# A two-layer decoder block: another issue order, another layout of the up-projection and narrower operands in its first layer

## The chip, the cores and the metric

The kernel runs on one NeuronCore of a Trainium2 chip. The metric is the device time of one execution in microseconds (us), lower is better.

## The reference

The input x has 16 sequences of 128 tokens of 256 features. Two layers follow each other, each an attention and a feed-forward part with a gate in front of its result. Only the first layer (layer 0) matters for this change:

```python
x = x + tanh(g_xattn[0]) * _L0_xattn_ref(_layernorm(x), ctx, causal, padding, Wq, bq, Wk, bk, Wv, bv, Wo, bo)
x = x + tanh(g_ffn[0])   * _L0_ffn_ref(_layernorm(x), w_up, w_down)
...
# attention: 32 query heads of 8 features, 8 key/value heads (groups) of 8 features, 128 x 128 scores
scores = einsum('bgrqd,bgkd->bgrqk', q, k) / sqrt(8)     # masked by causal and padding
out    = einsum('bgrqk,bgkd->bgrqd', softmax(scores), v)
# feed-forward: 256 -> 512 -> 256, both products on 8-bit activations and ternary weights
h = hbitlinear(x, w_up, 8);  h = square(relu(h));  return hbitlinear(h, w_down, 8)
# hbitlinear(x, w) = act_quant(fwht(x)) @ weight_quant(w).T ; fwht is a Walsh-Hadamard transform
```

Layer 1 is a second attention (16 heads of 128 features, self and cross, with values rounded to 8-bit floats) and a mixture of 8 experts, 2 for each token.

## The kernel before

**Stages.** Layer 0 goes over the 16 sequences ("tiles", index i). Its work on a tile is cut into pieces, functions with a short name and an engine. `ORDER0` holds, for each of the five engines, the order written out by hand in which it issues the pieces within one turn of the loop; a sign behind a name shifts the tile (`F6---` in the turn of tile i works on tile i-3, `P3++` on tile i+2), and the number behind a colon is the group g of heads. Each engine issues strictly in this order, and pieces wait for each other by semaphores. So a turn of each engine has the work of one whole tile, and the turns overlap like a pipeline. Turns at the two ends leave out pieces of tiles that don't exist. `MIXED` interleaves the last turns of layer 0 (letter a) with the first steps of layer 1's attention (b) and with the loading of its output weights (c). Behind it layer 1's loop, its routing and its experts follow.

**Pieces of attention.** P1, P2, P2t, P2a: normalise a row, transpose it (TensorE), copy it out. P3 (TensorE, L634 to L641): project v, k and q; `wk` is padded with zeros to 128 columns. P3h, P3v: bias, and a split of each number into two 16-bit halves. OUT, INS, INT, ROW (SyncE): send these parts through DRAM into the layouts that the score products need. S:g (L722, L723): the mask and the scores of group g, two products of 512 columns. MX:g (VectorE, L730): their maxima. NT, NTh, NTl: turn the maxima round; ROW puts them into rows 32 and 33 of `qT`. ST:g (L763, L764): the transposed scores minus the maxima, again a mask product and a product of `kT` with `qT`; both tiles have ROWS0 = 96 rows, of which rows 0 to 23 and 32 to 33 carry numbers and the others add zero. EX:g (ScalarE, L773): exponential. PV:g (L785): probabilities times values, fp32, a stationary operand of 32 columns that stands at columns 32 (g mod 4) of the array:

```python
e.matmul(O[GP * j:GP * j + GP, :], v1[:, p, g, :], prob[:, g % RING0, :, :], start=True, stop=True,
         tile_position=(0, GP * j)).then_inc(pe_PV.sem, 1)
```

In the order before, PV:0 to PV:3 stand directly behind one another and NT behind them, and so do PV:4 to PV:7. OC, OB, NO: copy the result out, transpose, divide. OT, OTa, W, Wv: transpose, output projection, add to x.

**Pieces of the feed-forward part.** F1, F1g, F2, F2t, F2a: normalise and transpose (F2 is L859, F2t L867). F3b, F3, F3q: Hadamard transform and quantisation. F4, F4a: transpose of the 8-bit values. F4u (L946): the up-projection, weights stationary, in 8 products of 128 columns, so that its result is transposed already. F4s: relu and square into `hid`. F5v (GpSimd): two butterflies of the 512-wide transform, the second one written to `hidT`. F6 (L974) to F7v (L1016): the rest of the transform, quantisation, down-projection, add to x.

**Preparing layer 1's weights.** LW, WM, WC, WH, WL load and scale one unit of them in each turn; WL (L1056) and WC (L1043, L1046) are long operations on GpSimd.

**Start.** Groups of loads are tied to pieces: the piece `rest` of ScalarE, 22 DMA issues, stands ahead of P2a of tile 2, and the load of the last twelve sequences ahead of CT of tile 2.

Of the kernel before, what the change touches and what calls it, by code (L numbers as in the profile page):

```python
# [252 lines left out]
def make_more_constants(e, t, made):  # L253
# [21 lines left out]
ROWS0 = 96  # L275
# [15 lines left out]
    "gpsimd": "XB+ F5v-- F1g- MK++ WL+ F3b- VC++ PD+ P1g++++ WC++ F7s-- F4v-",
    "sync": "INS- ROW-- INT- LW OUT CT++",
# [3 lines left out]
def layer0(nc, a, t, ctx):  # L296
# [10 lines left out]
    wq, wk, wv = sb("wq0", [P, KD, D]), sb("wk0", [P, KD, P]), sb("wv0", [P, KD, G0 * HD0])  # L307
# [632 lines left out]
    def _(e, i, p):  # L940
# [10 lines left out]
    def _(e, i, p):  # L951
# [3 lines left out]
        e.wait_ge(g_fly.sem, g_fly.at(i - 1))  # L955
# [3 lines left out]
    def _(e, i, p):  # L959
# [106 lines left out]
    def starting(owner, last):  # L1066
# [3 lines left out]
            ("gpsimd", "P1g", 1, 1): ("blocks",), ("gpsimd", "MK", 0, 0): ("ready",), ("gpsimd", "XB", 0, 0): ("gated",),  # L1070
# [10 lines left out]
    def bounds(owner):  # L1081
# [5 lines left out]
             "v_nl": v_nl, "v_max": v_max, "a_exp": a_exp, "v_part": v_part, "v_o": v_o, "a_q1": a_q1, "v_x2": v_x2, "d_out": d_out}  # L1087
# [98 lines left out]
def layer1_attention(nc, a, t, ctx, bank, places, final, small):  # L1186
# [331 lines left out]
    def _(e, i, b, j, kind):  # L1518
# [3 lines left out]
        if first(i):  # L1522
            spent(e, ("a_q1", "v_x2")[kind])
# [207 lines left out]
def routing(nc, a, t, s, flags, A, S, places, packet, rest_halves):  # L1731
# [295 lines left out]
    for b0, b1 in GROUPS[SOON:]:  # L2027
# [25 lines left out]
    "sync": "aaaaaaaaaaaaabaccccbccbcc",
# [354 lines left out]
```

## Time and profile before

| | us |
|---|---|
| median of 3 runs | 1297.82 (1297.1 to 1300.01) |
| profiled execution, its own time | 1297.1 |
| its span | 1295.3 |
| busy: TensorE matmul, weight load | 1172.4 (91%), 930.4 (72%) |
| busy: VectorE, ScalarE, GpSimd | 1059.1 (82%), 908.2 (70%), 748.6 (58%) |
| last F7v (end of layer 0) starts at | 363.8 |

Of the time of an execution 1.8 us lie outside the span. Matmuls in a row overlap in the profile, so the distance between two starts tells what one costs, not its duration. PE is TensorE, DVE VectorE, ACT ScalarE, POOL GpSimd, SP SyncE.

### The profile page before, as it was taken

How to read it: one execution, taken by the hardware profiler on the slowest of the kernel's cores; microseconds unless marked ns; L12 is line 12 of the kernel's file. 1: busy time of each engine (PE TensorE's matmuls, PEld its weight loads, DVE VectorE, ACT ScalarE, POOL GpSimd, SP SyncE). 2: the span in 40 equal slices, each digit the busy share in tenths (PEclk: the TensorE clock that was granted, in tenths of full speed). 3: DMA queues.
4: the chain of work that ended last, by engine and by line, in shares of the span. 5: the costliest groups of instructions: out<-in, count | busy, mean ns of one | idle time of the engine just before them, and what ended most of it. 6: DMA issues, size and time to landing. Idle time of an engine off the chain costs nothing. (4 is left out here: it accounts for less than half of the span.)

```text
span 1295.3 us, 30618 instructions
## 1 busy us (share of the span) xinstructions
PE 1172.4 (91%) x8917; PEld 930.4 (72%) x8917; DVE 1059.1 (82%) x2479; ACT 908.2 (70%) x3605; POOL 748.6 (58%) x1099
## 2 busy tenths in 40 slices
PE   2599999988899999999999999998999999399992
PEld 2256655644588888888888888886887788279992
DVE  6479999988798888988888899897788887656664
ACT  1166666657899899989989988997888787123331
POOL 3457777776756655665665666565556786313331
PEclk9699999999899999999999999999999999689996
DMA  7444444442130202220220221122211000722325
GB/s 171 92 87 90 90 88 82 82 79 47 56 117 2 87 18 69 86 69 17 86 86 0 86 86 36 50 86 85 71 50 55 30 34 21 293 75 77 90 83 195
DMA packets 145817, 100.47 MB, mean 78 GB/s; under 512 B 68541, under 2 KB 139198, under 8 KB 145728
## 3 DMA queue, kind: packets, MB, share of 16 engines
q1 hardware_dynamic: 134592, 87.28, 26.1%
q0 software_dynamic: 3744, 8.45, 1.8%
q10 hardware_dynamic: 7392, 3.64, 1.0%
q8 instruction: 44, 0.72, 0.2%
q14 instruction: 45, 0.37, 0.1%
HBM read 58.42 MB, written 42.48 MB: 78 GB/s over the span
## 5 line engine op out<-in xcount | busy, mean ns | idle before, releaser
L1418 POOL TENSOR_TENSOR head_rstd<-head_rstd,minus_half 128x4 f32<-128x4 f32 x192 | 223.8, 1166 | 15.1
L1406 ACT ACTIVATE squares<-ps 128x128 bf16<-128x128 f32 x768 | 202.0, 285 | 43.1 <-PE ps L1369 35.8
L1369 PE MATMUL ps<-w_proj_in,xq 128*128 128x512 f16 (+1 forms) x1024 | 210.4, 328 | 6.0 <-ACT headsT L1442 5.4
L1498 POOL TENSOR_TENSOR prob<-prob,rinv 128x512 f32<-128x512 f32 x128 | 140.4, 1098 | 108.5 <-DVE rinv L1493 108.3
L1442 ACT ACTIVATE headsT<-ps,l_hln 128x256 f32<-128x256 f32 (+1 forms) x256 | 168.2, 691 | 30.1 <-PE ps L1433 30.1
L1485 ACT ACTIVATE prob<-ps,nmax 128x128 f32<-128x128 f32 x512 | 182.2, 391 | 10.0 <-DVE nmax L1476 8.5
L1406 ACT ACTIVATION_READ_ACCUMULATOR squares<-ps 128x1 f32 x768 | 165.5, 216 | 0.0
L1426 DVE TENSOR_TENSOR heads_n<-ps,head_rstd 128x512 f32<-128x512 f32 x192 | 131.4, 684 | 25.5 <-POOL head_rstd L1418 25.4
L1369 PEld LDWEIGHTS ps<-w_proj_in,xq 128*128 (+1 forms) x1024 | 100.1, 98 | 53.9 <-issue 9.1
L1469 PE MATMUL ps<-headsT 128*128 128x128 f32 x1024 | 136.6, 277 | 1.0 <-DVE probT L1514 0.4
L1416 POOL TENSOR_TENSOR head_rstd<-head_squares,l_head_eps 128x4 f32<-128x4 f32 x192 | 47.1, 246 | 153.0 <-ACT squares L1406 152.1
L1469 PEld LDWEIGHTS ps<-headsT 128*128 128x128 f32 x1024 | 128.7, 192 | 8.0 <-issue 5.4
L1525 PE MATMUL ps<-probT,v 128*128 128x256 f32 x512 | 132.2, 381 | 0.3 <-DVE x_rows L1016 0.3
L1574 PE MATMUL ps<-w_proj_out,catq 128*128 128x256 f16 x1024 | 122.7, 273 | 3.9 <-DVE catq L1562 3.8
L1433 PE MATMUL ps<-ident,heads_n 128*128 128x128 f32 x768 | 117.1, 275 | 6.5 <-DVE heads_n L1426 6.4
L1485 ACT ACTIVATION_READ_ACCUMULATOR prob<-ps,nmax 128x1 f32 x512 | 118.0, 230 | 0.0
L1476 DVE TENSOR_REDUCE nmax<-ps 128x4 f32<-128x512 f32 x128 | 88.2, 689 | 28.8 <-PE ps L1469 27.0
L1574 PEld LDWEIGHTS ps<-w_proj_out,catq 128*128 128x128 bf16 x1024 | 100.3, 98 | 15.4 <-DVE catq L1562 4.4
L1433 PEld LDWEIGHTS ps<-ident,heads_n 128*128 128x128 f32 x768 | 91.3, 142 | 24.3 <-DVE heads_n L1426 16.7
L1376 PE MATMUL ps<-w_proj_in,ctx_parts 128*128 128x256 f16 x768 | 105.0, 273 | 0.0
L730 DVE TENSOR_REDUCE nmax<-ps 128x4 f32<-128x512 f32 x128 | 84.1, 682 | 24.6 <-PE ps L723 21.9
L2271 POOL DMA_INDIRECT picked<-slots_y,to_row x46 | 44.9, 975 | 99.7 <-ACT slots_y L2261 92.3
(302 smaller groups left out, 2772.3 us busy)
## 6 DMA issues: line engine op xcount, KB each, us to landing
slots<-blank_slot SPq DMA_DIRECT2D x12, 1554.0 KB, 8.5
halves<-half_made SPq DMA_DIRECT2D x32, 256.0 KB, 2.5
w_proj_in<-halves SPq DMA_DIRECT2D x16, 512.0 KB, 10.0
taken<-slots SPq DMA_DIRECT2D x23, 259.0 KB, 3.4
w_out_raw<-in_wprojT SPq DMA_DIRECT2D x8, 512.0 KB, 3.9
half_raw<-in_winT SPq DMA_DIRECT2D x16, 256.0 KB, 2.9
half_raw<-in_woutT SPq DMA_DIRECT2D x16, 256.0 KB, 3.1
q_stack<-q_parts SPq DMA_DIRECT2D x48, 64.0 KB
```

The lines of the kernel that those rows point to most:

```text
L1369: last = e.matmul(out, xq[:, k, which, slot_at], weights(k, hl, c0, n), start=(k == 0 and hl == 0), stop=(k == KD - 1 and hl == 1))
L1376: last = e.matmul(out, cx[:, k, part, slot_at], weights(k, hl, c0, n), start=(k == 0 and part == hl == 0), stop=(k == KD - 1 and part == 1))
L1406: last = e.activation(squares[:, 4 * n + h, :], A[n][:, h * HD1:(h + 1) * HD1], ACT.Square, scale=HD1**-0.5, accum_out=hss[:, 4 * n + h:4 ...
L1418: e.tensor_tensor(hr[:, four], hr[:, four], t["half"][:, four], ALU.pow).then_inc(g_r[n].sem, 1)
L1426: e.tensor_tensor(hn[:, n, :, :], A[n][:, :].rearrange("p (h d) -> p h d", h=4), spread(hr[:, 4 * n:4 * n + 4], HD1), ALU.mult).then_inc(v ...
L1433: last = e.transpose(A[n][:, h * P:(h + 1) * P], hn[:, n, h, :], ident[:, :])
L1442: last = e.activation(hT[:, n, h0:h1, :].rearrange("p h t -> p (h t)"), A[n][:, h0 * P:h1 * P], ACT.Identity, bias=hln[:, c + 1:c + 2], sc ...
L1469: last = e.matmul(S[kind][:, h * P:(h + 1) * P], hT[:, kind, h, :], hT[:, 2, 2 * kind + h // 2, :], start=True, stop=True)
L1485: last = e.activation(prob[:, kind, h, :], S[kind][:, h * P:(h + 1) * P], ACT.Exp, bias=nmax[:, kind, h:h + 1], accum_out=rowsum[:, kind, ...
L1498: e.tensor_tensor(prob[:, kind, :, :], prob[:, kind, :, :], spread(rinv[:, kind, :], P), ALU.mult).then_inc(g_p[kind].sem, 1)
L1525: last = e.matmul(O[kind][:, g * 2 * P:(g + 1) * 2 * P], v[:, kind, g, :], probT[:, kind, 2 * g:2 * g + 2, :], start=True, stop=True)
L1574: last = e.matmul(A[1][:, 0:D], catq[:, 4 * kind + h, :], wp[:, hl, 4 * j + 16 * kind + h, :], start=(n == 0), stop=(n == 15))
```

## The change

- `ORDER0` gets another order on all five engines. On TensorE, PV:4 and PV:5 stay together and the other six PV pieces of a turn stand alone between other products; NT stands alone; P2t moves from two to three tiles ahead.
- The up-projection F4u has the activations stationary: 2 products of 512 columns. Its result isn't transposed, so F5 (4 fp32 transposes into bank F0) and F5a (ScalarE copies 128x512 from there to `hidT`) are new, and F6 waits for F5a. F5v writes its second butterfly back to `hid`. The pieces that use bank F0 (F2t, and near the ends OT and W) wait for F5a as well; in layer 1 the first PV does.
- ROWS0 falls from 96 to 34, so the product of ST has 34 rows; `wk` has 64 columns without padding. Two memsets of 32 rows at the start become one of two rows, and that of `qT` covers 34 rows.
- The pieces that loads are tied to come in the new order: in ScalarE's, P2a of tile 2 stands directly behind P3h of tile 1, where it stood behind WH and NTh of tile 0. The wait for the gates on GpSimd moves from XB to PD.
- `MIXED` has new strings. On TensorE 25 steps of layer 1 stood ahead of layer 0's last piece, now 17.

The diff, cut: the entries `a_hT`, `pe_hT` in the lists of flags and the other strings of `MIXED` are left out.

```diff
-ROWS0 = 96
+ROWS0 = TOP + 2
 
 ORDER0 = {
     "tensor": (
-        "PV:2- PV:3- NT ST:5- P2t++ F6--- ST:6- OB:0- F2t-- ST:7- P3++ S:0+ F3-- PV:4- PV:5- PV:6- PV:7- ST:0 "
-        "S:1+ ST:1 S:2+ F4-- ST:2 OB:1- F4u-- S:3+ ST:3 S:4+ OT- ST:4 S:5+ F7--- W- S:6+ S:7+ F7d--- PV:0 "
-        "PV:1"
+        "S:7 F5--- ST:4- ST:5- OB:0- NT F6--- P3++ F2t-- ST:6- PV:4- PV:5- ST:7- PV:6- S:0+ F3-- PV:7- "
+        "ST:0 ST:1 S:1+ OB:1- S:2+ F4-- ST:2 ST:3 F4u-- PV:0 OT- PV:1 S:3+ S:4+ PV:2 S:5+ F7--- W- "
+        "P2t+++ S:6+ PV:3 F7d---"
     ),
     "scalar": (
-        "EX:5 P2a+++ F2a- EX:6 EX:7 P3h+++ OC:1 EX:0+ EX:1+ F4a- EX:2+ F4s- OTa WH++ F7a-- EX:3+ NTh++ EX:4+ "
-        "OC:0+"
+        "WH EX:7- P3h++ OC:1- EX:0 EX:1 F4a-- EX:2 F4s-- OTa- EX:3 F7a--- OC:0 P2a+++ F5a-- EX:4 NTh+ "
+        "EX:5 F2a- EX:6"
     ),
     "vector": (
-        "MX:5+ Wv- MX:6+ MX:7+ F1- F7v--- WM++ NTl+ F2- F6q-- NO:0 P1++++ MX:0++ F3q- P3v+++ MX:1++ MX:2++ "
-        "NO:1 MX:3++ MX:4++ P2++++"
+        "F2-- NO:0- NTl F6q--- WM+ P1+++ MX:0+ F3q-- NO:1- P3v++ MX:1+ MX:2+ P2+++ MX:3+ MX:4+ MX:5+ Wv- "
+        "F1- MX:6+ F7v--- MX:7+"
     ),
-    "gpsimd": "XB+ F5v-- F1g- MK++ WL+ F3b- VC++ PD+ P1g++++ WC++ F7s-- F4v-",
-    "sync": "INS- ROW-- INT- LW OUT CT++",
+    "gpsimd": "XB WC F5v--- F4v--- F1g-- MK+ F3b-- F7s--- WL VC+ P1g+++ PD+",
+    "sync": "ROW- INT CT++ OUT+ LW+ INS+",
 }
...
-    wq, wk, wv = sb("wq0", [P, KD, D]), sb("wk0", [P, KD, P]), sb("wv0", [P, KD, G0 * HD0])
+    wq, wk, wv = sb("wq0", [P, KD, D]), sb("wk0", [P, KD, G0 * HD0]), sb("wv0", [P, KD, G0 * HD0])
...
-            e.dma_start(wk[:, k, 0:G0 * HD0].rearrange("p (g d) -> p g d", g=G0), one_head).then_inc(w_first, 16)
+            e.dma_start(wk[:, k, :].rearrange("p (g d) -> p g d", g=G0), one_head).then_inc(w_first, 16)
...
         e.memset(kT[0:TOP, :, :, :].rearrange("p s g t -> p (s g t)").bitcast(F32), 0.0)
-        for r0 in range(TOP, ROWS0, 32):
-            e.memset(kT[r0:r0 + 32, :, :, :].rearrange("p s g t -> p (s g t)"), UP)
+        e.memset(kT[TOP:ROWS0, :, :, :].rearrange("p s g t -> p (s g t)"), UP)
         e.wait_ge(x_in[0], 16)
 
     @s.piece("ready", "vector")
     def _(e):
-        e.memset(wk[:, :, G0 * HD0:P], 0.0)
...
         for k in range(KD):
-            e.matmul(X[:, k_at:k_at + P], wk[:, k, :], cT[:, p, k, :],
+            e.matmul(X[0:G0 * HD0, k_at:k_at + P], wk[:, k, :], cT[:, p, k, :],
                      start=(k == 0), stop=(k == KD - 1))
...
@@ OT and W (tensor): the waits for the bank F0, outside the loop @@
-        filling(e, i, (a_yT, -1), (v_x1, -1))
+        filling(e, i, (a_yT, -1), (a_hT, -2), (v_x1, -1))
...
-        filling(e, i, (a_q1, -1), (a_yT, -1))
+        filling(e, i, (a_q1, -1), (a_yT, -1), (a_hT, -2))
...
@@ F2t (tensor) @@
         e.wait_ge(f_yn.sem, f_yn.at(i))
+        e.wait_ge(a_hT.sem, a_hT.at(i - 1))
         filling(e, i, (v_x1, 0), (a_oT, 0), (a_q1, -1))
...
@@ F4u (tensor) @@
-        for m in range(KF):
-            for k in range(KD):
-                last = e.matmul(F1[:, m * P:(m + 1) * P], wup[:, k, m * P:(m + 1) * P], q1T[:, k, :],
-                                start=(k == 0), stop=(k == KD - 1))
+        for k in range(KD):
+            last = e.matmul(F1[:, :], q1T[:, k, :], wup[:, k, :], start=(k == 0), stop=(k == KD - 1))
...
@@ F4s (scalar) @@
-        e.wait_ge(g_fly.sem, g_fly.at(i - 1))
+        e.wait_ge(pe_hT.sem, pe_hT.at(i - 1))
...
@@ F5v (gpsimd), F5, F5a, F6 @@
+        e.tensor_tensor(hid[:, 0:2, :], fly[:, 0:2, :], fly[:, 2:4, :], ALU.add)
+        e.tensor_tensor(hid[:, 2:4, :], fly[:, 0:2, :], fly[:, 2:4, :], ALU.subtract).then_inc(g_fly.sem, 1)
+
+    @s.piece("F5", "tensor")
+    def _(e, i, p):
+        e.wait_ge(g_fly.sem, g_fly.at(i))
+        if not isinstance(i, int) or i + 1 < B:
+            e.wait_ge(v_x1.sem, v_x1.at(i + 1))
+        filling(e, i, (a_oT, 1), (a_q1, 0), (a_yT, 0))
+        for k in range(KF):
+            last = e.transpose(F0[:, k * P:(k + 1) * P], hid[:, k, :], ident[:, :])
+        last.then_inc(pe_hT.sem, 1)
+
+    @s.piece("F5a", "scalar")
+    def _(e, i, p):
+        e.wait_ge(pe_hT.sem, pe_hT.at(i))
         e.wait_ge(pe_h2.sem, pe_h2.at(i - 1))
-        e.tensor_tensor(hidT[:, 0:2, :], fly[:, 0:2, :], fly[:, 2:4, :], ALU.add)
-        e.tensor_tensor(hidT[:, 2:4, :], fly[:, 0:2, :], fly[:, 2:4, :], ALU.subtract).then_inc(g_fly.sem, 1)
+        e.activation(hidT[:, :, :].rearrange("p k t -> p (k t)"), F0[:, :], ACT.Copy).then_inc(a_hT.sem, 1)
 
     @s.piece("F6", "tensor")
     def _(e, i, p):
-        e.wait_ge(g_fly.sem, g_fly.at(i))
+        e.wait_ge(a_hT.sem, a_hT.at(i))
...
@@ PV of layer 1, first step @@
-            spent(e, ("a_q1", "v_x2")[kind])
+            spent(e, ("a_hT", "v_x2")[kind])
...
@@ MIXED["tensor"], layer 0 (a) and layer 1 (b) at the handover @@
-        "aaaaaaaaaaaaaaaaaaaaaaaaaaaaaaaabaaaaaaaaaabaaaaaaaaaaaaaaaaaaabaaaaaaaaaaabbaaaaabaaababaaabbababab"
-        "ababbbbabababbbbababbbbbbbbbbbbbbbbbbbbbbbbbbbbbbbbbbbb"
+        "aaaaaaaaaaaaaaaaaaaaaaaaaaaaaaaaaaaaaaaaaaaaaaaaaaaaaaaaaaaaaaaaaaaaaaaaaaaaaaaaaaaaaaaaaaaaaaaaaaaa"
+        "aaaaaaaaaaaaaaaaaaaaaaaaaaaaaaaaaaaaaaaaaaaaaaaabaaaaaaaaabaaaaaaababaabbaababbabbaabbbaabbbabbbbbbb"
+        "bbbbbbbbbbbbbbbbbbbbbbbbbbbbbbbbbbbbb"
```

## Rows read from the trace of the kernel before

**Rows 1.** Stretches of 40 us: length, busy (instructions) of each engine, clock, DMA, GB/s.

```profile
core 0: us, PE busy (x) PEld busy (x) DVE busy (x) ACT busy (x) POOL busy (x), PEclk, DMA share, GB/s
40.00:80.00 40.00, 27.80 (x140) 13.96 (x140) 22.13 (x47) 13.92 (x27) 16.79 (x21) 0.78 0.44 83
...
160.00:200.00 40.00, 38.46 (x262) 23.24 (x261) 37.05 (x96) 25.46 (x50) 30.87 (x51) 1.00 0.46 91
...
280.00:320.00 40.00, 33.18 (x203) 17.53 (x202) 35.09 (x101) 24.73 (x49) 25.99 (x47) 0.91 0.26 57
```

**Rows 2.** Timeline of PE, 180 to 200 us: start, duration, line, operation, count.

```profile
180.75 0.60 PE L1009 MATMUL ps<-wdn,q2T 128*128 128x256 bf16 x4
181.28 1.07 PE L785 MATMUL ps<-prob,v_ones 128*32 128x512 f32 x8
182.28 0.28 PE L736 MATMUL ps<-ident,nmax 128*32 128x128 f32 x1
182.40 0.38 PE L763 MATMUL ps<-minus,causal_b 128*128 128x512 bf16 x1
182.61 0.38 PE L764 MATMUL ps<-q_rows,k_rows 96*128 96x512 f16 x1
...
184.48 0.60 PE L798 MATMUL ps<-ident,o_cols 128*128 128x128 f32 x4
186.16 0.44 PE L867 MATMUL ps<-ident,yn 128*128 128x128 f32 x2 [1.08 <-DVE yn L859]
...
189.63 1.06 PE L785 MATMUL ps<-prob,v_ones 128*32 128x512 f32 x8
190.62 0.39 PE L763 MATMUL ps<-minus,causal_b 128*128 128x512 bf16 x1
...
192.93 0.60 PE L798 MATMUL ps<-ident,o_cols 128*128 128x128 f32 x4
193.37 0.61 PE L946 MATMUL ps<-q1T,wup 128*128 128x128 bf16 x8
193.86 0.39 PE L722 MATMUL ps<-mask,minus 128*128 128x512 bf16 x1
...
196.50 1.08 PE L834 MATMUL ps<-wo,oT 128*128 128x256 f32 x4
197.41 0.38 PE L722 MATMUL ps<-mask,minus 128*128 128x512 bf16 x1
...
198.29 0.60 PE L1009 MATMUL ps<-wdn,q2T 128*128 128x256 bf16 x4
```

**Rows 3.** Timeline of DVE, same stretch.

```profile
183.91 2.20 DVE L859 SCALAR_TENSOR_TENSOR yn<-x_rows,mv_f,rstd_f 128x256 f32<-128x256 f32 x1
...
196.00 0.48 DVE L597 SCALAR_TENSOR_TENSOR xn<-x_rows,mv_p,rstd_p 128x256 f32<-128x256 f32 x1
```

**Rows 4.** Timeline of POOL, same stretch.

```profile
183.69 2.13 POOL L1056 TENSOR_TENSOR w_proj_in<-unit_raw,w_proj_in 128x1024 f32 x1
```

**Rows 5.** PE by source line L785: duration min/median/max in ns, first and last start.

```profile
L785 PE MATMUL ps<-prob,v_ones x256: 592/617/1062, 65.6 to 331.1; 128*32 128x512 f32 x128
```

**Rows 6.** Timeline of ACT at the start.

```profile
44.23 5.92 ACTq L399 DMA_DIRECT2D wo<-in_WoT  x16
...
53.26 0.38 ACT L617 ACTIVATE xnT<-ps 128x256 f32<-128x256 f32 x1 [8.77 <-issue]
```

**Rows 7.** Timeline of PE at the start.

```profile
53.78 1.08 PE L634 MATMUL ps<-wv,cT 128*128 128x64 f32 x4 [9.17 <-ACT xnT L617]
...
57.33 0.51 PE L722 MATMUL ps<-mask,minus 128*128 128x512 bf16 x1
```

**Rows 8.** Timeline of SP at the start.

```profile
44.93 1.39 SPq L692 DMA_DIRECT2D k_blocks<-k_parts  x4
46.41 1.24 SPq L755 DMA_DIRECT2D q_rows<-most_rows  x2
```

**Rows 9.** Stretches of 7 us where the granted clock falls.

```profile
283.00:290.00 7.00, 3.94 (x18) 1.84 (x15) 6.14 (x25) 1.79 (x3) 3.10 (x7) 0.73 0.27 59
290.00:297.00 7.00, 6.41 (x32) 2.94 (x31) 5.14 (x16) 3.31 (x7) 4.86 (x8) 0.78 0.02 5
```

**Rows 10.** Groups by line and shape, 160 to 240 us: busy, mean ns of one.

```profile
L792 ACT ACTIVATE o_cols<-ps 128x512 f32<-128x512 f32 x9 | 5.3, 590 | 5.8 <-PE ps L785 5.8
```

More of the change, by code:

```diff
@@ L553, in layer0 @@
     v_q1, g_two, pe_q1, a_q1 = sig("v_q1", "vector"), sig("g_two", "gpsimd", 2), sig("pe_q1", "tensor"), sig("a_q1", "scalar")
-    pe_up, a_hid = sig("pe_up", "tensor"), sig("a_hid", "scalar", 2)
+    pe_up, a_hid, pe_hT = sig("pe_up", "tensor"), sig("a_hid", "scalar", 2), sig("pe_hT", "tensor")
     g_sum, g_fly, g_scale = sig("g_sum", "gpsimd"), sig("g_fly", "gpsimd", 2), sig("g_scale", "gpsimd")
-    pe_h2, v_q2 = sig("pe_h2", "tensor"), sig("v_q2", "vector")
+    a_hT, pe_h2, v_q2 = sig("a_hT", "scalar"), sig("pe_h2", "tensor"), sig("v_q2", "vector")
     pe_q2, a_q2, pe_dn, v_x2 = sig("pe_q2", "tensor"), sig("a_q2", "scalar"), sig("pe_dn", "tensor"), sig("v_x2", "vector")
@@ L927, in _ @@
         e.wait_ge(a_yT.sem, a_yT.at(i))
-        filling(e, i, (v_x1, 0), (a_oT, 0))
+        filling(e, i, (a_hT, -1), (v_x1, 0), (a_oT, 0))
         for k in range(KD):
@@ L1069, in starting @@
             ("scalar", "P3h", 0, 0): ("weights",), ("scalar", "P2a", 1, 1): ("gated",), ("scalar", "P2a", 2, 0): ("rest",),
-            ("gpsimd", "P1g", 1, 1): ("blocks",), ("gpsimd", "MK", 0, 0): ("ready",), ("gpsimd", "XB", 0, 0): ("gated",),
+            ("gpsimd", "P1g", 1, 1): ("blocks",), ("gpsimd", "MK", 0, 0): ("ready",), ("gpsimd", "PD", 0, 0): ("gated",),
             ("tensor", "P3", 0, 0): ("ready",), ("tensor", "S", 0, 0, 0): ("late",), ("tensor", "W", 0, 0): ("out",), ("tensor", "F3", 0, 0): ("made",),
@@ L1086, in layer0 @@
     final = {"pe_qkv": pe_qkv, "pe_S": pe_S, "pe_ST": pe_ST, "pe_PV": pe_PV, "pe_OB": pe_OB, "g_mask": g_mask, "g_ulow": g_ulow,
-             "v_nl": v_nl, "v_max": v_max, "a_exp": a_exp, "v_part": v_part, "v_o": v_o, "a_q1": a_q1, "v_x2": v_x2, "d_out": d_out}
+             "v_nl": v_nl, "v_max": v_max, "a_exp": a_exp, "v_part": v_part, "v_o": v_o, "a_hT": a_hT, "v_x2": v_x2, "d_out": d_out}
     layer = Layer(s, lambda owner: starting(owner, bounds(owner)[0]), lambda owner: some(owner, bounds(owner)[1], B + B), turn,
@@ L2040 @@
     "tensor": (
-        "aaaaaaaaaaaaaaaaaaaaaaaaaaaaaaaabaaaaaaaaaabaaaaaaaaaaaaaaaaaaabaaaaaaaaaaabbaaaaabaaababaaabbababab"
-        "ababbbbabababbbbababbbbbbbbbbbbbbbbbbbbbbbbbbbbbbbbbbbb"
+        "aaaaaaaaaaaaaaaaaaaaaaaaaaaaaaaaaaaaaaaaaaaaaaaaaaaaaaaaaaaaaaaaaaaaaaaaaaaaaaaaaaaaaaaaaaaaaaaaaaaa"
+        "aaaaaaaaaaaaaaaaaaaaaaaaaaaaaaaaaaaaaaaaaaaaaaaabaaaaaaaaabaaaaaaababaabbaababbabbaabbbaabbbabbbbbbb"
+        "bbbbbbbbbbbbbbbbbbbbbbbbbbbbbbbbbbbbb"
     ),
     "vector": (
-        "aaaaaaaaaaaaaaaaaabbaaaaaaaaaaaaaabaaabaaaaaaaabaaaaabbbabbbaaaabaababbacbaaacaabbbabbbbbcbcbabbabbb"
-        "abbbbbbbbcbbbbbbbbcbbbbbbbbbbbbbbbbcbbbbbbbbbbbcbbbbbbb"
+        "aaaaaaaaaaaaaaaaaaaaaaaaaaaaaaaaaaaaaaaaaaaaaaaaaaaaaaaaaaaaaaaabbaababaababcaabcbbbbaaacababbabbccb"
+        "abbbabbbbbbabcbbbbbbbbbbbbbbbbbbbbbbbbbbbbbbbbbbbbbbbbbbbbbbbbbbbcbbcb"
     ),
     "scalar": (
-        "aaaaaaaaaaaaaaaaaaaaaaaaaaaaaaaaabbbaaaabaaabaaabaabaabbaabcaaaabaabababaababccbbbacbbbbabababbbccbb"
-        "babbbbbbbbbbcbbbbbbbbcbbbbbb"
-    ),
-    "gpsimd": "aaaaaaaaaaaabaaaaaaaaaaabaaaaaaabbaababababaababaabbbabbabbbbbbbbbbbbbbbbbbbbbbbb",
-    "sync": "aaaaaaaaaaaaabaccccbccbcc",
+        "aaaaaaaaaaaaaaaaaaaaaaaaaaaaaaaaaaaaaaaaaaaaaaaaaaaaaaaaaaaaaaaaaaaacacaaabaabbbabbababaabacbabbabbb"
+        "ccabababbabbbbbabcbbbbbbbbbbbbbbbbbbbbbbbbbbbbbbcc"
+    ),
+    "gpsimd": "aaaaaaaaaaaaaaaaaaaaaaaaaaaaaaaaaaaaaaaaaaaababaabbaaabbaabbaabbabbbbbbbbbbbbbbbbbbbbbbbbbbbbb",
+    "sync": "aaaaaaaabcccbcccccb",
 }
```

## The prediction

> **What bounds the kernel now.** I read the stretches of 40 us first, because the change touches layer 0 alone, which ends near 364 us. In its middle PE is busy for 38.46 of 40 us, DVE for 37.05, ACT and POOL for far less [rows 1]. So two engines are near their limit and the timelines must decide. In PE's the same product comes round from 180.75 to 198.29 us, a turn of 17.54 us [rows 2]. The only gap in it stands ahead of F2t: the four transposes of OB start at 184.48 and four such cost 0.44 us (192.93 to 193.37), the next start is 186.16, so 1.24 us are lost and 16.3 us are work. The gap ends with F2 on DVE, which takes 2.20 us there where the like of it takes 0.48 us [rows 3]; WL of POOL runs for 2.13 us at that time [rows 4]. So DVE is as full as PE only because one operation of it is held up, and behind it PE has a queue of work that barely fits. PE's work in a turn is what I sum.
>
> **PV alone.** A fp32 product of 256 columns costs 0.23 us (four from 196.50 to 197.41), so one of 512 columns some 0.45 us, and a PV is two such instructions, 0.91 us. The eight instructions of four PVs would be 3.6 us in a row; they take 0.99 us from their first start to the next product (189.63 to 190.62) [rows 2]. Four PVs stand at different columns of the array and run side by side; a block lasts as long as one of them. Going in costs a little more: four products at 0.11 us (half the 0.22 us of 512 columns) from 180.75 should end at 181.18, the block starts at 181.28, 0.10 us later; and 0.99 is 0.08 us over 0.91. So a block costs 1.09 us, whether it holds four or one. Before there are 2 in a turn. In the new order there are 7: PV:4 with PV:5, then PV:6, 7, 0, 1, 2 and 3, each with full-width products between, which need the columns that the lone PV uses. Five more blocks are +5.45 us. NT had its place behind a block in the same form (32 columns) and now pays for going in and out itself: 0 to 0.2 us, I take 0.15.
>
> **Switches of form.** The 0.10 us before and 0.08 us behind a block are the one price that the rows show for a change of the form in which the array is used. The product of ST goes from 96 to 34 rows, between products of 128. The trace has no product with 64 rows or fewer; those of 96 rows pay nothing (0.22 us in a row with 128 rows, 182.61 against 182.40) [rows 2]. Its bounds are 0 and, by the block of 32 columns, 0.18 us, 8 times in a turn: 0 or +1.45 us. I take the upper end, as 34 rows fit into half of the array like 32 columns into a quarter, and 96 don't; that is a guess from the nearest row. The Trainium skill (TensorEngine Tiling (Array Packing), Key Properties) says that changing the tiling mode drains the engine, and lists 64 rows as a mode of its own; the block of 32 columns agrees with it (0.10 and 0.08 us), and by that rule these are the +1.45 us. The page TensorE: Matmul & The Clock Gate of the Trainium skill (LDWEIGHTS) says that the number of rows makes no difference to a weight load; by that alone it would be 0.
> `wk` with 64 columns is between +0.2 us (a switch) and -0.2 us (four loads of half the width); I take 0.
>
> **The feed-forward part.** F5 is four fp32 transposes, +0.44 us like OB's. F4u takes 0.49 us now (193.37 to 193.86) and two products of 512 columns take 0.43: -0.05. F5a is one more ACT copy of 128x512, 0.59 us [rows 10] on an engine that is busy for 25.46 of 40 us; with PE's turn over 20 us it is hidden. If it were not, PE would wait at F6, but OB, NT and two STs (2.2 us) stand between F5 and F6. F5v is the same work to another tile.
>
> **The sum of a turn:** 5.45 + 0.15 + 1.45 + 0.44 - 0.05 = +7.45 us, from 16.3 to 23.8 us of PE work. DVE (37.05 of 40 us, so 16.3 us of a turn with the held-up F2 in it) then has 7 us of slack, POOL more. So F2's hold-up, which the new order may end (WL now stands behind F3b and F7s, and F2 waits for F1g alone), saves nothing. I followed the waits round one turn with the durations above (maxima to S two groups later; F3q to F4; OC to OB; F5v to F5; NT by ROW's two transfers to ST:0): each has more PE work in front than it lasts, the narrowest ROW with 2 us to spare. 16 tiles: +119 us.
>
> **What is taken off.** PE's idle time is filled. From the first S of tile 1 (57.33) [rows 7] to the last PV instruction (331.1) [rows 5] are 274 us. Work in them: 16 x 16.3 = 261 us, less some 19 of first and last pieces outside, plus 4 of layer 1's steps, 246 us; so 28 us idle, of which 6.8 lie in 280 to 320 us [rows 1]. I estimate that 10 remain (start, and turns near the end with less work): -18 us.
> The start: the 22 issues of `rest` hold ACT until 53.26, 8.77 us, and P3 of tile 2 and S:0 of tile 1 behind it start at 53.78 and 57.33 [rows 6, 7]. In the new order `rest` follows P3h of tile 1, which is done at 27 us, when ACT has nothing to do. S:0 of tile 1 then waits for INS, whose last issue starts at 44.93 for 1.39 us [rows 8]; LW stands before it now (six issues, 2.7 us). I expect it near 50 us: -7 us; bounds -9 and 0.
> The handover: layer 0's last tile has F5 and F5a in its chain, 1.4 us with their waits, and 8 steps of layer 1, about 6 us of PE work that filled gaps, come after it. Some of that overlaps: +6 us.
>
> **Sum:** 119 - 18 - 7 + 6 = +100 us on the profiled execution's 1297.1 us, which is 0.7 us under the median: **1398 us** for a median.
>
> **Rivals.**
> A, narrow rows are free. The product of 34 rows costs what 96 did. For it: 96 rows cost the same as 128. Against it: what 32 columns pay. 119 falls by 23 to 96 us: 1375 us. Chance 0.22.
> B, the clock. Half-clock stretches appear where PE waits: 0.73 and 0.78 between 283 and 297 us behind a gap of 3 us [rows 9]. Five blocks more in which a quarter of the columns works could let it fall in the middle of layer 0, where it is 1.00 now [rows 1]. Against it: PE never rests. If a tenth of the 380 us of PE work ran at 1.2 instead of 2.4 GHz, +38 us: 1436 us. Chance 0.10.
> C, the other side: a lone PV doesn't block. If full-width products start in the other columns while a PV runs, as other PVs do, six lone PVs cost little over their share of a block (0.25 us), and a turn is 16.3 + 0.44 + 0.15 + 1.45 = 18.3 at most; without the switches 16.9, under today's 17.54. With the hold-up of F2 gone the period falls by 0.3 us and the start by 7: 1286 us. It decides where a lone PV costs under 0.4 us. Against it: the product behind a block starts 0.99 us after it, never within it. Chance 0.05.
> D, another wait in the new order (ROW or F5v late) comes on top of PE's work, 1 to 2 us a turn: 1415 us. Chance 0.08.
> The forecast itself: 0.55, with a range of its own of 1380 to 1415 us.
>
> **How the numbers follow.** The range takes the forecast, A and D with the bounds of the start and the idle time, and leaves out C and most of B: 1355 to 1422 us. About 0.2% is what a measurement can tell from no change. Only C isn't slower: 0.04 for faster and 0.01 for within 0.2%, where its parts are eaten up; the other four are slower, 0.95.
>
> **What would show it.** In the profile after, layer 0 ends near 463 us and a turn of PE is near 23.8 us without gaps over 1 us; each lone PV takes 1.0 to 1.1 us from start to next start; ST's second product is followed or preceded by 0.1 us more than S's; ACT has no `rest` issues at 44 us; busy DVE falls to two thirds in the middle. Layer 1 and the experts are as before. Wrong would be: lone PVs under 0.5 us, a turn that ends with a wait of PE for another engine, a granted clock under 1.00 in the middle of layer 0.

## The result and the profile after

The changed kernel takes 1393.47 us (median of 4 runs, 1390.16 to 1395.96), the kernel before beside it 1298.91 (1297.1 to 1302.65). The ratio is 1.072, with a 95% interval of 1.0697 to 1.0742. The profiled execution took 1393.06 us, its span is 1390.6, so 95.3 us more than before.

I read the stretches first, for they answer whether PE became the only bound. Changed kernel, columns as in [rows 1]:

```profile
160.00:200.00 40.00, 40.00 (x178) 16.73 (x177) 26.08 (x70) 20.66 (x39) 24.52 (x39) 1.00 0.35 71
```

PE is busy for 40.00 us of 40 with 178 matmuls where it had 262; DVE fell from 37.05 to 26.08 us [rows 1]. PE is full, with fewer instructions, so each must cost more. Timeline of PE in the changed kernel, which answers to [rows 2] (its lines are 1 or 2 lower up to F5 and 12 higher behind it; L783 is PV, L761 and L762 are ST, L720 and L721 are S, L734 is NT, L632 to L639 are P3, L944 is F4u, L971 F5, L1021 F7d):

```profile
237.24 0.28 PE L929 MATMUL ps<-ident_b,q 128*128 128x128 bf16 x2
237.35 0.38 PE L761 MATMUL ps<-minus,causal_b 128*128 128x512 bf16 x1
237.66 0.39 PE L762 MATMUL ps<-q_rows,k_rows 34*128 34x512 f16 x1
237.99 0.39 PE L761 MATMUL ps<-minus,causal_b 128*128 128x512 bf16 x1
238.31 0.39 PE L762 MATMUL ps<-q_rows,k_rows 34*128 34x512 f16 x1
238.62 0.60 PE L944 MATMUL ps<-wup,q1T 128*128 128x512 bf16 x2
239.16 1.05 PE L783 MATMUL ps<-prob,v_ones 128*32 128x512 f32 x2
240.14 0.44 PE L817 MATMUL ps<-ident,o_rows 128*128 128x128 f32 x2
240.50 1.04 PE L783 MATMUL ps<-prob,v_ones 128*32 128x512 f32 x2
241.48 0.39 PE L720 MATMUL ps<-mask,minus 128*128 128x512 bf16 x1
...
245.77 1.04 PE L783 MATMUL ps<-prob,v_ones 128*32 128x512 f32 x2
246.75 0.61 PE L1021 MATMUL ps<-wdn,q2T 128*128 128x256 bf16 x4
...
247.63 0.60 PE L971 MATMUL ps<-ident,hid 128*128 128x128 f32 x4
248.07 0.38 PE L761 MATMUL ps<-minus,causal_b 128*128 128x512 bf16 x1
...
249.83 0.27 PE L734 MATMUL ps<-ident,nmax 128*32 128x128 f32 x1
249.94 1.06 PE L986 MATMUL ps<-had,hidT 128*128 128x128 f32 x8
250.83 0.56 PE L632 MATMUL ps<-wv,cT 128*128 128x64 f32 x4
251.32 0.65 PE L635 MATMUL ps<-cT,wk 128*64 128x128 f32 x4
...
252.90 0.38 PE L866 MATMUL ps<-ident,yn 128*128 128x128 f32 x2
...
253.74 1.05 PE L783 MATMUL ps<-prob,v_ones 128*32 128x512 f32 x4
254.73 0.39 PE L761 MATMUL ps<-minus,causal_b 128*128 128x512 bf16 x1
...
270.41 0.61 PE L1021 MATMUL ps<-wdn,q2T 128*128 128x256 bf16 x4
```

A turn, from F7d to F7d, is 270.41 - 246.75 = 23.66 us, and no start in it has an idle time beside it. A lone PV (two instructions) holds PE for 0.98 us (239.16 to 240.14, 240.50 to 241.48), the pair (four) for 0.99 (253.74 to 254.73), as eight did before. The steps between ST's products are 0.31, 0.33, 0.32 and 0.31 us (237.35 to 238.62) where they were 0.21 to 0.22.

The start, in the timelines of ACT and PE, answers to [rows 6, 7]; the last three rows are PV, F7v (L1028) and F2 (L857) by source line, with their first and last start:

```profile
25.36 4.91 ACTq L399 DMA_DIRECT2D wo<-in_WoT  x14
```

```profile
41.28 0.66 PE L632 MATMUL ps<-wv,cT 128*128 128x64 f32 x4 [0.66 <-DMA cT<-in_ctxT]
...
49.30 0.61 PE L720 MATMUL ps<-mask,minus 128*128 128x512 bf16 x1 [5.08 <-DMA k_blocks<-k_parts]
```

```profile
L783 PE MATMUL ps<-prob,v_ones x256: 592/617/1061, 56.6 to 413.3; 128*32 128x512 f32 x128
...
L1028 DVE SCALAR_TENSOR_TENSOR x_rows<-ps,quant,x_rows x16: 464/484/484, 129.1 to 452.2; 128x256 f32<-128x256 f32 x10, 128x256 f32 x6
L857 DVE SCALAR_TENSOR_TENSOR yn<-x_rows,mv_f,rstd_f x16: 466/475/486, 84.8 to 424.3; 128x256 f32<-128x256 f32 x16
```

The first S of tile 1 starts 8.0 us earlier (49.30 against 57.33). Layer 0 ends 88.4 us later (452.2 against 363.8) and the span 95.3, so 6.9 us arise behind it. F2 (L857) takes 486 ns at most; its hold-up [rows 3] is gone, and the turn is longer all the same.

### The profile page after: what moved, and what is told of

Read it like the earlier page. It is cut to its first block and busy times, and to the rows that moved or that the text cites. A ratio compares the mean times of both kernels' runs of the same rounds, so it can differ in the third digit from the quotient of the medians.

```text
span 1390.6 us, 30539 instructions
## 1 busy us (share of the span) xinstructions
PE 1286.4 (93%) x8885; PEld 938.2 (67%) x8885; DVE 1054.3 (76%) x2477; ACT 925.3 (67%) x3621; POOL 743.8 (53%) x1099
## 5 line engine op out<-in xcount | busy, mean ns | idle before, releaser
L1438 DVE TENSOR_TENSOR heads_n<-ps,head_rstd 128x512 f32<-128x512 f32 x192 | 131.3, 684 | 25.0 <-POOL head_rstd L1430 24.8
L783 PE MATMUL ps<-prob,v_ones 128*32 128x512 f32 x256 | 116.0, 612 | 0.1
```

The costliest lines, as they stand in the source:

```text
L1438: e.tensor_tensor(hn[:, n, :, :], A[n][:, :].rearrange("p (h d) -> p h d", h=4), spread(hr[:, 4 * n:4 * n + 4], HD1), ALU.mult).then_inc(v ...
```

## The experiments

Each run has the kernel before beside it (medians 1298.45 to 1299.14 us). Every ratio is to that.

**Wide operands again**, in the changed kernel: `ROWS0 = 96`, `wk` of 128 columns with its padding.

> The changed kernel with only the narrow operands undone: ROWS0 is 96 again, wk has 128 columns with zeros, the memsets of before are back. Theory 1 (TensorE's work sets the turn, and each change of form costs 0.1 us each way): in the trace after, the mask product to ST's product takes 0.32 us and ST's product to the next one 0.32 us, against 0.22 with 96 rows, and wk's four stand 0.09 us later at both ends. That is 8 x 0.20 + 0.18 = 1.8 us a turn, 29 us for 16 tiles, less 1 to 3 us for the longer memsets at the start: 1364 to 1368 us. Theory 2 (the new order's waits set the turn and not TensorE's work): the time stays within 5 us of 1393.

Measured: 1365.01 us, ratio 1.0513 (1.0484 to 1.0541), 28.5 us less than the changed kernel. A turn of PE is 21.92 us here (239.24 to 261.16, from PV:6 to PV:6) against 23.66, and 16 times the difference of 1.74 us is 28 us. The narrow operands cost what the switches add up to; rival A is out.

**66 rows instead of 34**, `wk` left narrow:

```diff
-ROWS0 = TOP + 2
+ROWS0 = 66
```

> The changed kernel with ROWS0 66 instead of 34, and nothing else: rows 34 to 65 add zeros. In the changed kernel's trace a product of 34 rows costs 0.10 us more on its way in and 0.10 us on its way out than S's of 96 rows, 8 times a turn and 16 turns, 25.6 us. Theory 1 (the product is slow because it fits into half of the array's rows and the array changes its form for it): 66 rows don't fit, the 25.6 us go, 1366 to 1370 us. Theory 2 (any product with another number of rows than its neighbour pays, or pays by how few they are): 1380 us or more. a_wide took back 34 rows and 64 columns together and gave 28.5 us, so what is left of it to the 64 columns of wk is 28.5 less this run's gain: some 3 us by the trace's 0.18 us a turn.

Measured: 1368.69 us, ratio 1.0539 (1.0514 to 1.0563), 24.8 us less. Timeline of PE in this run:

```profile
234.91 0.61 PE L1022 MATMUL ps<-wdn,q2T 128*128 128x256 bf16 x4
...
236.67 0.38 PE L762 MATMUL ps<-minus,causal_b 128*128 128x512 bf16 x1
236.88 0.38 PE L763 MATMUL ps<-q_rows,k_rows 66*128 66x512 f16 x1
237.10 0.60 PE L797 MATMUL ps<-ident,o_cols 128*128 128x128 f32 x4
...
257.10 0.61 PE L1022 MATMUL ps<-wdn,q2T 128*128 128x256 bf16 x4
```

Steps of 0.21 and 0.22 us: 66 rows cost what 128 cost, 34 cost 0.1 us more on each side. So it isn't that neighbours differ in rows. A turn is 22.19 us (234.91 to 257.10), 1.47 less than with 34 rows; the other 0.27 us of the 1.74 belong to `wk`. At which number between 34 and 66 the price begins wasn't tried. The Trainium skill (TensorEngine Tiling (Array Packing), Key Properties) says that changing the tiling mode drains the engine; 34 against 66 rows agrees with it, if 34 rows run in a mode of fewer rows than 66.

**Narrow operands in the kernel before**, the reverse of the first run, so `ROWS0 = TOP + 2` and `wk` of 64 columns.

> The kernel before with only the narrow operands of the change: ROWS0 34, wk of 64 columns, the memsets of after. Theory 1: 1.8 us of TensorE work more in a turn that has 1.2 us of idle time in it, so +10 to +25 us: 1308 to 1323 us, ST's product starts 0.32 us behind its mask product. Theory 2 (VectorE sets the turn before, switches are hidden under it): within 5 us of before, 1294 to 1304 us.

Measured: 1318.17 us, ratio 1.0145 (1.0117 to 1.0172), +19.0. The same operands cost 28.5 us where PE is full and 19.0 where a turn has waits. Part of the difference is seen: between 120 and 280 us PE waits for other engines and for loads for 6.3 us in the kernel before and for 4.1 here. The rest wasn't traced.

**PV pieces apart in the kernel before**, seven blocks in a turn instead of two, all else as it was:

```diff
-"PV:2- PV:3- NT ST:5- ... S:0+ F3-- PV:4- PV:5- PV:6- PV:7- ST:0 ... S:6+ S:7+ F7d--- PV:0 PV:1"
+"PV:2- ST:5- PV:3- NT ... S:0+ PV:4- PV:5- F3-- PV:6- ST:0 PV:7- ... S:6+ PV:0 S:7+ PV:1 F7d---"
```

> The kernel before with only TensorE's order altered so that the PVs stand in 7 blocks instead of 2 (PV:4 with PV:5, the other six alone, NT behind PV:3), nothing else. Theory 1: 5 x 1.07 = 5.35 us of work more in a turn, 86 us for 16 tiles, of which 15 to 20 us fill idle time: 1361 to 1373 us. Theory 2 (a product of full width can run beside a lone PV): under +20 us, and in the trace a product that follows a lone PV starts less than 0.5 us behind it.

Measured: 1364.33 us, ratio 1.0498 (1.0469 to 1.0527), +65.2. Stretch of this run:

```profile
160.00:200.00 40.00, 39.99 (x214) 19.83 (x216) 28.74 (x78) 21.84 (x44) 25.92 (x42) 1.00 0.30 65
```

PE full, DVE down to 28.74 us: this edit alone makes the picture of the changed kernel in its middle. Five blocks by 1.07 us and 16 tiles are 86 us. The 20 us that are missing went into idle time by this sum, as the expectation had it (15 to 20).

**PV pieces together in the changed kernel**, in two blocks of four, the rest of the new order kept:

```diff
-"... ST:6- PV:4- PV:5- ST:7- PV:6- S:0+ F3-- PV:7- ... F4u-- PV:0 OT- PV:1 ... PV:2 S:5+ ... S:6+ PV:3 F7d---"
+"... ST:6- ST:7- S:0+ F3-- PV:4- PV:5- PV:6- PV:7- ... F4u-- OT- ... S:5+ ... S:6+ PV:0 PV:1 PV:2 PV:3 F7d---"
```

> The changed kernel with only TensorE's order altered so that PV:4 to PV:7 stand together where PV:7 stood, and PV:0 to PV:3 where PV:3 stood; narrow operands, F5 and all other engines as after. Theory 1 (a lone PV costs as much as a block of four): five blocks fewer at 1.07 us, so a turn falls from about 23.6 to 18.3 us of TensorE work, 86 us for 16 tiles: 1305 to 1315 us, and up to 1325 if other waits show when the turn is that short. Theory 2 (it is the narrow operands and the longer feed-forward chain that cost, PV little): less than 30 us are gained, 1365 us or more.

Measured: 1358.87 us, ratio 1.0461 (1.0433 to 1.049), only 34.6 us less. That is 34 us above the far end (1325 us) of what I had expected, and nearly 50 above its middle. Timelines of PE, DVE and POOL of this run:

```profile
240.67 0.39 PE L720 MATMUL ps<-mask,minus 128*128 128x512 bf16 x1 [1.59 <-DVE nmax L728]
...
252.66 1.75 PE L783 MATMUL ps<-prob,v_ones 128*32 128x512 f32 x8
...
261.62 0.39 PE L720 MATMUL ps<-mask,minus 128*128 128x512 bf16 x1 [1.57 <-DVE nmax L728]
```

```profile
238.34 1.67 DVE L595 SCALAR_TENSOR_TENSOR xn<-x_rows,mv_p,rstd_p 128x256 f32<-128x256 f32 x1
```

```profile
236.29 1.47 POOL L1055 TENSOR_TENSOR unit_raw<-unit_raw,unit_sum 128x768 f32<-128x768 f32 x1
237.84 1.90 POOL L1058 TENSOR_TENSOR unit_raw<-unit_raw,l_wscale 128x1024 f32<-128x1024 f32 x1
```

The turn is 261.62 - 240.67 = 20.95 us, 2.7 shorter and not 5.4. PE waits 1.57 us for a maximum, and one block takes 1.75 us instead of 1.06. It waits in its middle for the last exponential: ACT computes that from 252.64 to 253.32 us, and the block's last two weight loads start at 253.37. The maximum seems late because P2 on DVE (L595) takes 1.67 us, where it takes 0.47 unhindered (in the changed kernel its median is 1.12, and PE's work hides it); it ends 0.3 us behind the second operation of WC on POOL (L1058, to 239.7). Of the 16 x 2.7 = 43 us only 34.6 arrive, so some are lost again at the two ends of the layer.

**That hold-up taken away:** the same order, with WC behind MK on GpSimd.

```diff
-"XB WC F5v--- F4v--- F1g-- MK+ F3b-- F7s--- WL VC+ P1g+++ PD+"
+"XB F5v--- F4v--- F1g-- MK+ WC F3b-- F7s--- WL VC+ P1g+++ PD+"
```

> The changed kernel with the PV pieces in two blocks of four (as in the run with them together, 1358.87 us) and WC (1.47 and 1.90 us on GpSimd) moved from the front of GpSimd's turn to behind MK, where GpSimd has nothing to do for 6 us. In that run PE waited 1.6 us a turn for the maxima, because P2 on VectorE took 1.67 us instead of 0.47 while WC ran. Theory 1 (that hold-up is the wait): P2 takes 0.47 us, the wait falls to about 0.4 us, 16 turns by 1.2 us, 1338 to 1343 us. Theory 2 (the chain S, maximum, next S is too long by itself in that order): 1353 to 1359 us. If WC now holds up F2 instead and F2t is late for it: between.

Measured: 1341.56 us, ratio 1.0343 (1.0315 to 1.0371), 17.3 us less than without it. P2 by source line, and PE's longest waits between 120 and 280 us (total, times, longest):

```profile
L595 DVE SCALAR_TENSOR_TENSOR xn<-x_rows,mv_p,rstd_p x8: 465/468/469, 132.5 to 271.0; 128x256 f32<-128x256 f32 x8
```

```profile
PE ps L720 <- DVE nmax L728: 3.1, 8, 0.4
```

P2 takes 0.47 us again and the longest wait fell from 1.57 to 0.4 us: theory 1. The wait in the block's middle for the exponential stays, 0.6 us a turn.

**Together and wide**, both edits in the changed kernel.

> The changed kernel with both of the big costs taken back: ROWS0 96 and wk 128 columns as before, and the single PV pieces gathered into two blocks of four. Alone the first gave 28.5 us and the second 34.6. Theory 1 (with the PV pieces together a turn of 20.95 us holds 18.3 us of PE work and 2.6 us of waits that hang on PE's order, so what the wide operands save comes off in full): 1325 to 1335 us. Theory 2 (a chain through VectorE and GpSimd sets that turn, and PE's savings only lengthen its waits): 1350 to 1359 us. Between them both hold in part. If neither wait existed, the sum of a turn (16.3 + 0.44 + 0.15 - 0.05) would give some 1300.

Measured: 1334.39 us, ratio 1.0282 (1.0254 to 1.031). 59.1 us less than the changed kernel, where the two alone gave 28.5 and 34.6 (63.1 together): they add nearly in full, theory 1. It still stays 35.9 us above the kernel before. WC stands in its old place in this run, and between 120 and 280 us PE waits for maxima for 4.6 us in all and for POOL's butterflies ahead of F3 for 2.6. A run with all three edits wasn't made, so how the 35.9 us divide stays open.

**The up-projection as before** in the changed kernel. F5 and F5a are empty, F5v writes to `hidT` again and the waits for F5a are gone; of the edit only F4u is shown:

```diff
-        for k in range(KD):
-            last = e.matmul(F1[:, :], q1T[:, k, :], wup[:, k, :], start=(k == 0), stop=(k == KD - 1))
+        for m in range(KF):
+            for k in range(KD):
+                last = e.matmul(F1[:, m * P:(m + 1) * P], wup[:, k, m * P:(m + 1) * P], q1T[:, k, :],
+                                start=(k == 0), stop=(k == KD - 1))
```

> The changed kernel with the up-projection as before (weights stationary, 8 products, the result transposed already), F5 and F5a empty, the banks' waits as before; order, single PV pieces and narrow operands as in the changed kernel. My theory (PE is full, so each turn falls by 0.44 us of F5 less 0.05 of F4u, 16 times, and the last tile's chain by 1.4 us): 1384 to 1388 us, 6 to 9 faster than the changed kernel's 1393.5. Rival (F5's wait for F5v and F6's for F5a cost more than the products themselves): under 1380 us. Rival (the transposes fill time in which PE would wait anyway): within 2 us of 1393.5.

Measured: 1386.74 us, ratio 1.0683 (1.0658 to 1.0708). By the medians 6.7 us less, by the spans 5.9 (1384.7 against 1390.6), though the two ratios' intervals overlap. The expected 6 to 9 us fit, and no further cost of F5 shows.

**Only the early loads**, in the kernel before:

```diff
-("scalar", "P2a", 2, 0): ("rest",),
+("scalar", "WH", 0, 0): ("rest",),
```

> The kernel before, with the 22 DMA issues of `rest` tied to WH of tile 0 on ScalarE instead of P2a of tile 2, so that they stand behind P3h of tile 1 as in the new order. In the changed kernel's trace S:0 of tile 1 starts at 49.30 us where it started at 57.33. My theory (the start is worth what S:0 of tile 1 comes earlier, since PE is full from there): 5 to 8 us faster, 1291 to 1294 us. Rival 1 (the idle time is only moved: the first turns are set by VectorE and the loads, so the gain is lost by the middle): within 2 us of 1299. Rival 2 (the transfers of `rest` take the queues from CT and INS and these come later): slower by 2 us or more.

Measured: 1295.97 us (12 runs), ratio 0.9978 (0.9967 to 0.999), 2.5 us faster. The first S of tile 1 starts at 50.59 us, 6.7 earlier, but in the profiled execution layer 0's last F7v starts at 363.3 us, only 0.5 earlier. The timeline of PE in this run, and one stretch of it with columns as in [rows 1], show where the gain goes:

```profile
84.59 0.61 PE L722 MATMUL ps<-mask,minus 128*128 128x512 bf16 x1 [3.56 <-DMA k_blocks<-k_parts]
...
86.41 1.94 PE L785 MATMUL ps<-prob,v_ones 128*32 128x512 f32 x8
88.28 0.61 PE L763 MATMUL ps<-minus,causal_b 128*128 128x512 bf16 x1
```

```profile
81.00:88.00 7.00, 3.44 (x15) 1.44 (x14) 2.04 (x6) 0.87 (x3) 0.09 (x1) 0.67 0.29 53
```

In the kernel before the same S starts at 86.61 us, after 1.30 us of waiting for the same transfers, the granted clock stays at 1.00, and the product behind the block starts at 88.59. Here S starts 2.0 us earlier, after 3.56 us of waiting. The granted clock is 0.67 in this stretch, a mean of its two levels of 2.4 and 1.2 GHz, and the block takes 1.87 us (86.41 to 88.28) instead of 1.00, and 0.3 us are left. So the gain is lost in a wait for INS and at half the clock behind it, not to a full DVE: DVE is busy for 30.84 us of 40 between 80 and 120 us, less than the 33.73 before.

**WL kept away from F2**, and the early loads:

```diff
+        if not isinstance(i, int) or i >= 2:
+            e.wait_ge(f_yn.sem, f_yn.at(i - 2))
```

> b_early with one more wait: WL on GpSimd (2.13 us) starts only when F2 of the tile two before is done, so that the two can't run at the same time. In the kernel before F2 takes 2.20 us on VectorE in that case and 0.48 us elsewhere, and PE waits 1.08 to 1.24 us a turn behind it. My theory (F2's hold-up is what leaves PE idle in the middle): the wait goes, up to 14 turns by 0.5 to 1.1 us, of which VectorE (37 of 40 us busy, 1.7 us a turn of it the hold-up) allows all; with b_early's gain 1276 to 1288 us. Rival (the turn is set by VectorE's own work or by GpSimd, which starts WL later and so F3b and F7s later): no more than b_early, 1291 to 1296 us, or slower than b_early by a few us.

Measured: 1299.31 us, ratio 1.0007 (0.9995 to 1.0018): the rival. Timelines of DVE and POOL of this run (L1058 is WL here):

```profile
168.50 0.46 DVE L859 SCALAR_TENSOR_TENSOR yn<-x_rows,mv_f,rstd_f 128x256 f32<-128x256 f32 x1
169.02 0.69 DVE L893 TENSOR_REDUCE quant<-ps 128x1 f32<-128x512 f32 x1
169.75 1.66 DVE L895 TENSOR_TENSOR quant<-quant 128x1 f32<-128x1 f32 x1
```

```profile
169.25 2.13 POOL L1058 TENSOR_TENSOR w_proj_in<-unit_raw,w_proj_in 128x1024 f32 x1 [0.59 <-DVE yn L859]
```

F2 takes 0.46 us, and the next operation without PSUM, on a single column, takes 1.66 us: it ends with WL at 171.4. In the kernel before the same happens in most turns, which the one turn of [rows 2 to 4] doesn't show. Its timelines of DVE and POOL one turn earlier:

```profile
166.88 0.46 DVE L859 SCALAR_TENSOR_TENSOR yn<-x_rows,mv_f,rstd_f 128x256 f32<-128x256 f32 x1
...
168.12 1.24 DVE L895 TENSOR_TENSOR quant<-quant 128x1 f32<-128x1 f32 x1
```

```profile
166.97 2.38 POOL L1056 TENSOR_TENSOR w_proj_in<-unit_raw,w_proj_in 128x1024 f32 x1
```

Of nine turns between 120 and 280 us F2 takes 2.20 us in three. In the other six it takes 0.46 us, starts just ahead of WL, and the column product is held up (1.23 to 1.36 us). So this edit took F2's hold-up out of a third of the turns and put the other kind into all of them.

**WL behind F3b** on GpSimd, where it has 3 us with nothing to do:

```diff
-"XB+ F5v-- F1g- MK++ WL+ F3b- VC++ PD+ P1g++++ WC++ F7s-- F4v-"
+"XB+ F5v-- F1g- MK++ F3b- WL+ VC++ PD+ P1g++++ WC++ F7s-- F4v-"
```

> The kernel before, with WL and F3b changed about in GpSimd's order and nothing else, so that WL (2.13 us) runs in the 3 us in which GpSimd waits for PV anyway. In b_both WL only moved its hold-up from F2 (0.46 us again) to the next operation of VectorE with two inputs in SBUF, the product of two single columns (1.66 to 1.80 us where it takes 0.16 us in the changed kernel), and the time stayed. My theory (a small or large operation of VectorE with two SBUF inputs waits for the whole operation of GpSimd that runs, and this is what makes a turn 17.5 us where PE has 16.3 us of work): neither F2 nor that column product stands in WL's time now, VectorE loses 1.6 us a turn, the turn falls to 16.4 to 16.9 us, and the kernel to 1283 to 1292 us. Rival (a loop of maxima, products and quantisation through VectorE and PE sets the turn, the hold-up lies in its slack): 1296 to 1301 us.

Measured: 1297.87 us, ratio 0.9988 (0.9974 to 1.0003), no change that can be told. Timelines of DVE, POOL and PE in this run:

```profile
187.85 0.16 DVE L895 TENSOR_TENSOR quant<-quant 128x1 f32<-128x1 f32 x1
...
189.47 2.42 DVE L904 TENSOR_SCALAR q<-rnd 128x512 bf16<-128x512 f32 x1
...
196.26 1.27 DVE L730 TENSOR_REDUCE nmax<-ps 128x4 f32<-128x512 f32 x2
```

```profile
189.47 2.13 POOL L1056 TENSOR_TENSOR w_proj_in<-unit_raw,w_proj_in 128x1024 f32 x1
...
195.37 1.47 POOL L1043 TENSOR_TENSOR unit_raw<-unit_raw,unit_sum 128x768 f32<-128x768 f32 x1
```

```profile
191.94 0.71 PE L889 MATMUL ps<-had,yfly 128*128 128x128 f32 x4 [1.14 <-DVE q L904]
```

The column product is quick (0.16 us), and now the copy to bf16 behind it takes 2.42 us (0.43 in the run above), although it reads one operand only: WL starts at the same 189.47 for 2.13 us. PE waits 1.14 us for it. The hold-up has moved to a third place. My theory was too narrow in its second operand, and whether the turn falls without any hold-up was not tried. The Trainium skill (SBUF — State Buffer, SBUF: two separate sides) says that VectorE and GpSimd share a pair of ports as an exclusive lock, taken by an operation of VectorE with two inputs in SBUF or in a two-port mode. The trace agrees with it for two inputs (F2, P2, the column product); the copy has one input and was held up too, but in which mode it ran the trace doesn't show. The maxima, which read PSUM, go on beside WC (L730, 1.27 us for two at 196.26, as elsewhere).

**Both, WL behind F3b and the early loads:**

> b_swap and b_early together. b_early alone gave 2.5 us (1295.97 against 1298.45), less than the 8 us by which its S:0 of tile 1 comes earlier, since VectorE fills the rest of the time. If the two add: 2 to 3 us under b_swap. If b_swap shortens the turn, PE and VectorE lose slack in which the late start was caught up, and b_early may give more, up to 6 us under b_swap. If b_swap gives nothing: 1296 us.

Measured: 1294.54 us (12 runs), ratio 0.9975 (0.996 to 0.999), against 1299.01. So a version faster than both kernels is there, by 0.25%. That the change of WL adds to the early loads isn't shown: the intervals of the two runs overlap. In the trace of this run PE waits 2.8 us for INS at the same place, and the granted clock is 0.91 and 0.85 in the two stretches of 7 us from 81 us on.

## Why the prediction was right

Predicted were 1398 us and a range of 1355 to 1422, measured 1393.47. By its terms:

| | predicted, us | measured, us |
|---|---|---|
| five more PV blocks, a turn | +5.45 | +5.35 (0.98 and 0.09 going in, 5 times) |
| NT alone | +0.15 | 0 (249.83 to 249.94, 0.11, a plain product's time) |
| ST of 34 rows | +1.45 | +1.47 (23.66 less the 22.19 with 66 rows) |
| wk of 64 columns | 0 | +0.27 (22.19 less the 21.92 with both wide) |
| F5, F4u | +0.44, -0.05 | +0.44, -0.04 |
| a turn of PE | 23.8 | 23.66 |
| 16 turns | +119 | +118 (16 x 7.36) |
| idle time filled | -18 | -21 (not read: what is left, 88.4 = 118 - 8 - 21) |
| start | -7 | -8 |
| handover | +6 | +7 (span less last F7v) |

The measured terms of a turn add up to 7.49 us, the turn grew by 7.36. The rest is in F6 and P2t: F6's eight products take 0.89 us (249.94 to 250.83) where they took 0.97 (183.08 to 184.05); why wasn't looked into. The 16.3 us of work come from one turn of 17.54 us. The turn ahead of it in the kernel before is 17.06 us long with a wait of 0.6 us ahead of F3, so its work is about the same.

- **PE's work decides.** Shown: PE is busy for 40 of 40 us, and putting PV apart in the kernel before is enough for +65 us. Rival C is out: a lone PV costs 0.98 us, a block of four 0.99.
- **Switches of form.** The guess from the nearest row held: 34 rows pay 0.1 us on each side. Where a PV follows directly, ST's way out and PV's way in are paid once (253.43 to 253.74, 0.31 us; 0.32 us with 96 rows). Rival A's bound of no cost was wrong, by both runs that take it away.
- **The small terms missed.** NT's transpose pays no switch where 32 columns of PV do, and `wk` pays more than one (P3 takes 2.07 us, 250.83 to 252.90, against 1.79 with 128 columns) where I had set a gain of the loads against it, of which the trace shows none. Set against the forecast, the two are 0.12 us a turn off, some 2 us in all; that two misses partly cancel is luck.
- **The clock** stays at 1.00 in the middle of layer 0, so rival B is out; no wait for another engine shows in a turn, so D is out too. So the new order of the other four engines costs nothing that can be seen in the middle; no run changes it by itself.
- **The end of layer 0** came at 452.2 us, not near 463. More idle time was filled than the 18 us that I had estimated, and the number in the text put the handover's 6 us before F7v, while the trace has 6.9 behind it. That these 6.9 us are the 8 steps of layer 1 is argued: no run puts the old `MIXED` back.
- **F2's hold-up was read from one turn.** That DVE was as full as PE only because of it holds for three turns of nine; in the others another operation of DVE waits for WL. The prediction gave it no worth in the new order, so nothing in its sum hangs on it.
- **The start** came 8.0 us earlier, but what that is worth there wasn't tested by itself; in the kernel before 6.7 us of it were worth 2.5.
- **What failed came later,** in what I expected of the run with PV together: the step from "five blocks cost 5.35 us a turn" to "without them 86 us come back". As a price it holds; as a saving it gave 34.6, because an order made around lone pieces has PE waiting for DVE and ACT when they are gone.

## What to carry to other kernels

Count an engine's work in a turn by the steps between starts, and count each change of the array's form (32 columns, 34 rows) as 0.1 us in and 0.1 us out (once where two such forms meet): small products that could run side by side in quarters of the array belong directly behind one another. Padding 34 rows to 66 made this kernel 24.8 us faster. A price read from a full engine is not yet what taking it away gives: waits hidden under it come out (here 34.6 us of 86). An earlier start is worth what is left of it behind the next wait; and an operation of VectorE that suddenly takes longer than its like is to be looked for beside GpSimd's long ones, all that follow included.

## What was not expected of the hardware

- The fp32 transpose with 32 columns (NT) has 0.11 us from its start to the next product's, alone between products of 128 columns; the fp32 product of 32 columns (PV) pays 0.09 us going in. What tells them apart wasn't tried.
- With the early loads in the kernel before, PE waited 3.56 us at one place and the granted clock was 0.67 in the 7 us around it; with 1.30 us of waiting at the same place it was 1.00.
- A product on a single column, 0.16 us by itself, took 1.64 to 1.80 us on VectorE beside GpSimd's WL, and a one-operand copy of 128x512 to bf16 2.42 instead of 0.43 us.
